# A graph network on one core: record scatters unrolled and split 224 and 168, attention weighing shared by ScalarE and VectorE

## The reference

```python
edge_index = stack([src, dst])
x = x + gin(layernorm(x), edge_index)   # agg = segment_sum(x[src], dst); 4 linear layers, batch norm and elu between
x = x + moe(layernorm(x))               # 8 experts, top 2, silu(h1) * h3, 256 -> 682 -> 256
x = x + gat(layernorm(x), edge_index)   # attention over the edges, 4 heads of 64
x = x + ffn(layernorm(x))               # the top half of the nodes by a learned weight, gelu, 256 -> 1024 -> 256

# gat, the part that the change touches most:
xw = h @ W;  el = xw @ Wl.T;  er = xw @ Wr.T
e = exp(leaky_relu(el[src] + er[dst], 0.2))
w = e / max(segment_sum(e, src), 1e-12)[src]
out[hd] = segment_sum(w[:, hd:hd+1] * xw[dst], src)   # for each of the 4 heads
```

## Time and profile before

| | |
|---|---|
| median of 3 runs | 2623.48 us (2622.04 to 2626.05) |
| the profiled execution | 2622.28 us |
| its span, first to last instruction | 2620.7 us |
| PE busy | 71% of the span |
| DVE busy | 57% |
| POOL busy | 56% |
| ACT busy | 24% |

### The profile page before, as it was taken

One profiled execution on the slowest core, in us unless ns is written; L12 is line 12 of the kernel. 1 busy time (PEld: TensorE's weight loads), 2 busy tenths in 40 slices (PEclk: granted clock), 3 DMA queues, 4 the chain that ended last, 5 costly groups with the idle time before them and its releaser, 6 DMA issues. The chain is left out here.

```text
span 2620.7 us, 37949 instructions
## 1 busy us (share of the span) xinstructions
PE 1861.2 (71%) x9564; PEld 1336.1 (51%) x9565; DVE 1496.4 (57%) x3214; ACT 631.6 (24%) x1252; POOL 1480.6 (56%) x1583
## 2 busy tenths in 40 slices
PE   3988889898979650405999996267788777731597
PEld 2766667743434340403666664256566656620366
DVE  7666544465567370471333333646666666668698
ACT  4000000025566340151333332121111111110343
POOL 3777777717777777174662002757777777751000
PEclk8555665588989875557999998568887888865699
DMA  7333333340000230321111111321111111120100
GB/s 219 106 102 104 104 105 104 105 139 1 1 1 1 74 113 1 128 72 55 37 37 37 39 36 41 89 59 25 26 25 25 25 25 25 25 12 0 25 24 26
DMA packets 112944, 144.01 MB, mean 55 GB/s; under 512 B 46660, under 2 KB 82372, under 8 KB 112764
## 3 DMA queue, kind: packets, MB, share of 16 engines
q0 software_dynamic: 60160, 86.81, 13.8%
q1 hardware_dynamic: 52729, 56.58, 7.0%
HBM read 114.00 MB, written 29.18 MB: 55 GB/s over the span
## 5 line engine op out<-in xcount | busy, mean ns | idle before, releaser
L1484 POOL DMA_INDIRECT g<-tab_d,recs x416 | 460.0, 1106 | 148.8 <-issue 126.5
L597 POOL DMA_INDIRECT rec_d<-str__1722,stp x392 | 393.2, 1003 | 172.5 <-issue 94.6
L497 PE MATMUL psA<-oh,G 128*128 128x128 f32 x1568 | 433.4, 438 | 73.6 <-DMA G<-xn_d,gat_i 35.7
L312 POOL DMA_INDIRECT G<-xn_d,gat_i x392 | 378.6, 966 | 145.0 <-issue 134.3
L497 PEld LDWEIGHTS psA<-oh,G 128*128 128x128 f32 x1568 | 340.4, 303 | 166.6 <-issue 93.2
L1625 PE MATMUL psS<-vv,oh 128*125 128x260 f32 x832 | 307.9, 523 | 128.6 <-DVE acc L1560 128.6
L1625 PEld LDWEIGHTS psS<-vv,oh 128*125 128x125 f32 x832 | 180.4, 245 | 222.1 <-DVE acc L1560 183.1
L825 PE MATMUL psZ<-z,W 128*128 (+1 forms) x1344 | 264.0, 359 | 27.0 <-DVE z L739 27.0
L447 DVE TENSOR_TENSOR accT<-accT,psA 128x256 f32 x392 | 165.0, 421 | 167.6 <-PE psA L497 141.6
L643 ACT ACTIVATE z<-psZ,vec 128x500 f32 (+2 forms) x112 | 70.8, 633 | 640.7 <-PE psZ L818 530.9
L1234 PE MATMUL psH<-we,xh 128*128 x1344 | 214.7, 310 | 0.5 <-issue 0.5
(11 more groups left out here) (253 smaller groups left out, 2728.4 us busy)
## 6 DMA issues: line engine op xcount, KB each, us to landing
raw<-in_L_ffn_w SPq DMA_DIRECT2D x16, 682.0 KB, 9.3
xs_d<-zero SPq DMA_DIRECT2D x1, 7168.0 KB, 23.9
xs<-xs_d SPq DMA_DIRECT2D x56, 128.0 KB, 2.0
y_d<-yv POOLq DMA_DIRECT2D x56, 128.0 KB, 2.0
g<-tab_d,recs POOLq DMA_INDIRECT x416, 2.5
G<-xn_d,gat_i POOLq DMA_INDIRECT x392, 2.7
rec_d<-str__1722,stp POOLq DMA_INDIRECT x392
raw<-in_L_ffn_w SPq DMA_DIRECT2D x16, 384.0 KB, 9.8
```

The lines of the kernel that those rows point to most:

```text
L312: pool.indirect_dma_start(out=G[:, i, :], out_offset=None, in_=xn_d, in_offset=bass.IndirectOffsetOnAxis(ap=gat_i[:, t:t + 1], axis=0)).th ...
L497: last = nc.tensor.matmul(psA[i // 2][:, i % 2, h, :], G[:, i, 128 * h:128 * (h + 1)], oh[:, i, :], start=True, stop=True)
L597: pool.indirect_dma_start(out=rec_d.rearrange("p (t r) -> (p t) r", r=2), out_offset=bass.IndirectOffsetOnAxis(ap=stp[:, h, j:j + 1], axis=0),
L1484: pool.indirect_dma_start(out=g3[:, n % BODY, j, :], out_offset=None, in_=tab_d, in_offset=bass.IndirectOffsetOnAxis(ap=recs[:, t, 1:2], a ...
```

## The change

In the MLP stage POOL issues 224 record DMAs straight from `posd` and `rec`, with no copies, no loop and no wait between them. The other 168 go into the expert stage, three behind each of the 56 stores, again straight from `posd` and `rec`. In the attention ScalarE weighs tiles 0 and 1 of each step (`weigh_first`, eight operations of 128x65 with a per-partition scale), VectorE tiles 2 and 3 in one operation of half the size. `scatter` waits for ScalarE's part first and for VectorE's ahead of tile 2; POOL waits for both before it fills the buffer again.

```diff
-        LATE = 12
+        EDGES_EARLY = 224
+        PER_TILE = (T1 - EDGES_EARLY) // T2
...
-            def stage(pool, g, h):
-                nc.gpsimd.tensor_copy(stp[:, h, :], posd[:, bass.ds(g * TPR + h * HT, HT)])
-                nc.gpsimd.tensor_copy(str_[:, h, :, :], rec[:, bass.ds(g * TPR + h * HT, HT), :]).then_inc(s_stg, 1)
-                pool.wait_ge(s_stg, g * 2 + h + 1)
-                pool.sem_inc(s_halves, 1)
-                for j in range(HT):
-                    pool.indirect_dma_start(
-                        out=rec_d.rearrange("p (t r) -> (p t) r", r=2),
-                        out_offset=bass.IndirectOffsetOnAxis(ap=stp[:, h, j:j + 1], axis=0),
-                        in_=str_[:, h, j, :], in_offset=None).then_inc(s_sc[h], 16)
+            def record(pool, t):
+                pool.indirect_dma_start(
+                    out=rec_d.rearrange("p (t r) -> (p t) r", r=2),
+                    out_offset=bass.IndirectOffsetOnAxis(ap=posd[:, t:t + 1], axis=0),
+                    in_=rec[:, t, :], in_offset=None).then_inc(s_sc[t % 2], 16)
...
-                stage(pool, 0, 0)
-                stage(pool, 0, 1)
-                with loop(nc, pool, 1, R1 - LATE) as g:
-                    for h in range(2):
-                        pool.wait_ge(s_sc[h], g * (16 * HT))
-                        stage(pool, g, h)
+                for t in range(EDGES_EARLY):
+                    record(pool, t)
...
-                with loop(nc, pool, 0, LATE) as g:
-                    for i in range(2):
-                        store(g * 2 + i, i)
-                        pool.wait_ge(s_sc[i], (g + (R1 - LATE)) * (16 * HT))
-                        stage(pool, g + (R1 - LATE), i)
-                with loop(nc, pool, LATE, T2 // 2) as g:
-                    for i in range(2):
-                        store(g * 2 + i, i)
+                for t in range(T2):
+                    store(t, t % 2)
+                    for j in range(PER_TILE):
+                        record(pool, EDGES_EARLY + t * PER_TILE + j)
...
                 for n in range(NS):
                     pool.wait_ge(s_V, n + 1)
+                    pool.wait_ge(s_Va, n + 1)
...
+                act.sem_inc(s_Va, 4)
+                def weigh_first(n, s):
+                    act.wait_ge(s_p, n + 1)
+                    act.wait_ge(s_sct, n + 3)
+                    for j in range(HT // 2):
+                        for h in range(NH):
+                            last = nc.scalar.activation(vv[:, s % 2, j, h * VW:(h + 1) * VW], g3[:, s, j, NH:RW], ACT.Copy,
+                                                        scale=pp[:, s % 2, j, h:h + 1])
+                    last.then_inc(s_Va, 1)
                 def step(n, s):
+                    if not isinstance(n, int) or n >= 0:
+                        weigh_first(n, s)
                     if not isinstance(n, int) or 0 <= n + 1 < NS:
                         exps(n + 1, (s + 1) % BODY)
                     if not isinstance(n, int) or 0 <= n + 3 < NS:
                         copy_turned(n + 3, (s + 3) % BODY)
...
-                        vv[:, s % 2, :, :].rearrange("p j (h f) -> p j h f", h=NH),
+                        vv[:, s % 2, HT // 2:, :].rearrange("p j (h f) -> p j h f", h=NH),
...
                 def scatter(n, s):
-                    pe.wait_ge(s_V, n + 5)
+                    pe.wait_ge(s_Va, n + 5)
                     for j in range(HT):
+                        if j == HT // 2:
+                            pe.wait_ge(s_V, n + 5)
```

More of the change, by code:

```diff
@@ L518, in program @@
         posd = at("posd", 1 * KB + 3136, [128, T1], I32)
-        stp = at("stp", 1 * KB + 4704, [128, 2, HT], I32)
-        str_ = at("str_", 1 * KB + 4736, [128, 2, HT, 2], I32)
-        LATE = 12
+        EDGES_EARLY = 224
+        PER_TILE = (T1 - EDGES_EARLY) // T2
+        assert EDGES_EARLY + PER_TILE * T2 == T1
         blk_d = dram("blk_d", (1, T3), I32)
@@ L533, in program @@
         s_blkst = sem("s_blkst")
-        s_stg = sem("s_stg")
         s_sc = [sem("s_sc0"), sem("s_sc1")]
@@ L981, in store @@
                 def store(t, i):
-                    wait_apart(pool, s_yv, 1 + t + 1, s_halves)
-                    pool.dma_start(y_d[bass.ds(t * 128, 128), :], yv[:, i, :]).then_inc(s_yst[i], 16)
-                with loop(nc, pool, 0, LATE) as g:
-                    for i in range(2):
-                        store(g * 2 + i, i)
-                        pool.wait_ge(s_sc[i], (g + (R1 - LATE)) * (16 * HT))
-                        stage(pool, g + (R1 - LATE), i)
-                with loop(nc, pool, LATE, T2 // 2) as g:
-                    for i in range(2):
-                        store(g * 2 + i, i)
-                for h in range(2):
-                    pool.wait_ge(s_sc[h], 16 * HT * R1)
+                    pool.wait_ge(s_yv, 1 + t + 1)
+                    pool.dma_start(y_d[t * 128:(t + 1) * 128, :], yv[:, i, :]).then_inc(s_yst[i], 16)
+                for t in range(T2):
+                    store(t, t % 2)
+                    for j in range(PER_TILE):
+                        record(pool, EDGES_EARLY + t * PER_TILE + j)
+                for i in range(2):
+                    pool.wait_ge(s_sc[i], 16 * (T1 // 2))
                 for i in range(2):
@@ L1339, in program @@
         s_V = sem("s_V")
+        s_Va = sem("s_Va")
         s_sct = sem("s_sct")
@@ L1549, in weigh @@
                     nc.vector.tensor_tensor(
-                        vv[:, s % 2, :, :].rearrange("p j (h f) -> p j h f", h=NH),
-                        g3[:, s, :, NH:RW].unsqueeze(2).to_broadcast([128, HT, NH, VW]),
-                        pp[:, s % 2, :, :].unsqueeze(3).to_broadcast([128, HT, NH, VW]), ALU.mult).then_inc(s_V, 1)
+                        vv[:, s % 2, HT // 2:, :].rearrange("p j (h f) -> p j h f", h=NH),
+                        g3[:, s, HT // 2:, NH:RW].unsqueeze(2).to_broadcast([128, HT // 2, NH, VW]),
+                        pp[:, s % 2, HT // 2:, :].unsqueeze(3).to_broadcast([128, HT // 2, NH, VW]), ALU.mult).then_inc(s_V, 1)
                 def accumulate(n, s, at_, tiles=range(HT)):
```

## The result

The changed kernel takes 2797.57 us (median of 4 runs, 2796.08 to 2799.98) where the kernel before takes 2624.77 (2622.04 to 2626.28) on the same chip: a ratio of 1.066, 95% interval 1.0642 to 1.0679. Its profiled execution took 2796.08 us, 2794.4 of it span.

The account below looks back on a forecast made before the run. It took POOL to bound the MLP stage's end, TensorE the expert stage, POOL narrowly the attention. 2620.7 - 88 + 4.3 + 236 = 2773 us of span, with 1.6 around it 2774.6; forecast 2775, range 2640 to 2890.

Parts of the forecast that it names:

- MLP stage, -88: End of the MLP stage: early records end before VectorE, so the next stage starts 88 us sooner (84 to 91).
- Expert stage, +4.3: Expert stage: records between stores cost nothing; the last three and their landing add 4.3 us.
- The ring, 6.0 and 9.1 us: Attention: scatter, pick, turn, copy, eight weighings, scatter form a closed chain, 6.0 us a step at full clock, 9.1 at half.
- The mix of the two, 7.95 a step: Attention: two half-clock steps for each full-clock one, 8.07 us, taken as 7.95 for mixed steps: +236 us.
- The clock stays high: Rival, attention: TensorE keeps full clock, 6.0 us a step, +33 us, 2572 us in all; chance 0.12.
- The clock stays low: Rival, attention: TensorE stays at half clock, 9.1 us a step, +356 us, 2894 us in all; chance 0.13.
- Hidden, and POOL gains: Rival, attention: weighing is hidden and gathers stretch less, 0.35 us a step, -36 us, 2502 us in all; chance 0.03.
- Not earlier: Rival, MLP stage: another queue holds its end, 88 us on top of the forecast, 2863 us; chance 0.03.

Follow-up runs that it names:

- e1: The changed kernel's record scatters with the attention of the kernel before: 2533.09 us, ratio 0.9647 to the kernel before.
- e8: e3 with 336 early record scatters and 56 behind the stores, in place of 224 and 168: 2585.07 us, ratio 0.9859.
- e4: The changed kernel with eight matmuls that nothing reads behind TensorE's turns in each attention step: 2569.5 us, ratio 0.9787.
- e3: The changed kernel with ScalarE weighing n+1 ahead of its copy of n+3: 2506.6 us, ratio 0.9551.
- e9b: e6 with five matmuls that nothing reads behind TensorE's turns: 3011.04 us, ratio 1.0645, where the kernel before takes 2827.43 us.
- e12: e3 with 280 early record scatters and 112 behind the stores: 3076.85 us, ratio 1.0978, where the kernel before takes 2796.12 us.
- e7: e3 with ScalarE weighing all four tiles and VectorE none: 2479.91 us, ratio 0.9449.
- e10b: The changed kernel with four matmuls that nothing reads behind TensorE's turns: 2993.93 us, ratio 1.0582, where the kernel before takes 2827.43 us.
- e6: The changed kernel with ScalarE weighing one tile of four and VectorE three: 2645.73 us, ratio 1.0093.

## Why the prediction was right

The forecast was 2775 us, the time 2797.57, in the range and on the side given 0.83. Step by step:

- **MLP stage, -88: right, -90.2 at its boundary.** The early records ended at 879.6 (forecast 887), since POOL began at 584.2 and a record cost 1.32 us; both were covered anyway. Leaving the block cost 0.33 us; I had bounded it by 0 and 6.2 and taken 3, which is the missing 2.7. e1 gives -92.5 for this part, e8 shows the rule from the other side.
- **Expert stage, +4.3: mis-sized, +0.9.** The records between the stores cost nothing, as said. The three behind the last store I had added to the store's landing, and from that store to the next stage it is 1.7 us more, not 4.3. I had left the end of the stage as long as before, but POOL's wait there is 3.77 us behind the last record where it was 7.26 behind the last store.
- **The ring, 6.0 and 9.1 us: right.** Its parts measured: TensorE to the copy 6.42 us at half clock (6.39 forecast), weighings 0.24 us apart (0.25), a gap of 2.68 (2.7). e4 gives 6.01 at full clock, the unfilled kernel 9.07 at half. By the Trainium skill, ScalarE: Activation LUTs, What ACT_TABLE_LOAD costs, an estimate for a weighing is 0.24 us; the trace agrees, as eight of 0.337 us take 2.02.
- **The mix of the two, 7.95 a step: mis-sized, 8.23, and this is the step that failed.** I took one step in three at 6.0. None was: the clock came back in the middle of a step, so that steps of 9.1 are followed by mixed ones of 7.4 to 8.0. The attention cost +268.1 instead of +236. The share was carried over from a kernel without the ring, and no row gave the 7.95 that I made of 8.07; that the time came within 1% of the forecast is in part luck, the ring and the way of the change are not. That a ring with a gap of 2.7 doesn't keep the clock held: of 101 scatters behind such gaps none ran at full clock throughout, and e4, with the gap filled, has the full clock. The Trainium skill, TensorE: Matmul & The Clock Gate, Why this matters for your kernels, warns only of idle gaps longer than this one; by that the gap should leave the clock high, and the rows disagree.
- **The rivals.** "The clock stays high" is the time of e4 (2569.5; I had 2572), where it was made to stay. "The clock stays low" (9.1 a step, 2894) did not come; the mean step, 8.23, lies between the forecast's 7.95 and it. "Hidden, and POOL gains" (2502; its rows, 4 x (1.106 - 0.944) halved, give 0.32 us a step and not 0.35, so 2505) is near the time of e3 (2506.6): it was the order of two calls away. "Not earlier" fell by the 90.2 us.
- **Not foreseen:** that variants of this kernel lose far more on some chips than the kernel before does (e9b to e12). Nothing in the trace of before spoke of it.

## What to carry to other kernels

Before you give an idle engine a share of the work, write down the ring that its new operation closes: what it stands behind in its engine's queue, and who waits for it before that can come again. The share itself was sound here: one place earlier in ScalarE's queue it takes 291 us less, and twice the share there less still (e7). A matmul engine that waits in every step can pay twice, for the wait and for the clock: most of the loss here (2.22 of 2.55 us a step) was the second, and a few matmuls that nobody needs took it back. Move work between two stages by the pace of the queue that carries it, and only as far as the other engines still outlast it.

## What the hardware showed that I had not expected

- **Two of the four chips of the experiments are slow at issue.** The kernel before takes 2796.12 and 2827.43 us there and 2621.99 to 2625.58 on the others. While POOL issues the early record scatters back to back in e12, the other engines get few instructions (TensorE busy 58 of 280 us). In e10b POOL began its records 96.3 us late (680.5 against 584.2) and from there the MLP stage took 648.7 us against 385.0, 264 more; the kernel before, whose 296 early records run in a loop, lost 202 us in all. If its first stage, the same in both, lost those 96 too, at most 106 are left for its MLP. That the written-out form is the cause follows from this sum alone and is argued, not shown: no trace of the kernel before was taken on these chips, nor was the changed kernel run there.
- **A matmul engine's gap of 1.7 to 1.8 us can go either way**: none of 101 scatters at full clock in e6, 83 of 84 in e10b, on another chip and with other work in the step.
- **A gather on POOL takes 944 ns in the median and 1117, 1040 or 981 ns on average** where POOL leads, as VectorE weighs four, two or no tiles beside it.
- **Leaving a block** costs 6.2 and 9.5 us when POOL's indirect DMAs end last, 0.33 us when VectorE does.
